# Decoder layer on one core: SyncE gets a list of its own, five x buffers in place of three, and new orders for the first stage

## The reference

```
x1  = layernorm(x  + attention(x))       # linear attention with a memory M, z; 128-wide head; causal sums
x2  = layernorm(x1 + convolution(ctx, x1))
out = layernorm(x2 + ffn(x2))            # y / rms(y) inside
```

```
kv = einsum('bhil,bhjl->bijhl', k_, v_)            # heads of 8, 32 heads
y  = irfft(rfft(kv) * rfft(ssm_kernel))[..., :L]   # causal convolution over L
out = einsum('bijhl,bhil->bjhl', y + kv * D, q_)
```

## Time and profile before

| | |
|---|---|
| median of 3 timed runs | 579.14 us (578.35 to 579.87) |
| the profiled execution | 574.02 us |
| its span, first to last instruction | 572.3 us |
| PE busy | 526.1 us, 92% of the span |
| ACT, POOL, DVE busy | 414.4 us (72%), 388.8 us (68%), 383.4 us (67%) |
| mean granted TensorE clock | 0.984 of full speed |

### The profile page before, as it was taken

How to read it: one execution, slowest core, us unless ns; L and a number is a source line. 1 busy time by engine, 2 the same in 40 slices (tenths; PEclk the granted TensorE clock), 3 DMA queues, 4 the chain that set the end, 5 groups by cost and what they waited for, 6 DMA issues and landing times.

```text
span 572.3 us, 11933 instructions
## 1 busy us (share of the span) xinstructions
PE 526.1 (92%) x3798; PEld 396.7 (69%) x3798; DVE 383.4 (67%) x1153; ACT 414.4 (72%) x978; POOL 388.8 (68%) x449
## 2 busy tenths in 40 slices
PE   5897997996999799999999999999999999998992
PEld 4686785875777467767876777687678767765660
DVE  3984665877776457787777768767877777763223
ACT  3474672535789568878897898788778968887980
POOL 2896762596287538976996798499769967972231
PEclk9998998999999899999999999999999999999997
DMA  9214233403022513012210311040121102001001
GB/s 234 74 52 140 74 115 107 129 1 92 2 75 88 133 50 98 3 57 77 89 47 11 110 55 55 20 145 0 55 81 65 37 0 75 2 1 37 2 19 37
DMA packets 26594, 36.44 MB, mean 64 GB/s; under 512 B 4474, under 2 KB 13818, under 8 KB 26554
## 3 DMA queue, kind: packets, MB, share of 16 engines
q1 hardware_dynamic: 26554, 35.94, 20.8%
HBM read 27.46 MB, written 8.47 MB: 63 GB/s over the span
## 4 chain that ended last, share of the span: by engine, by line
PE 78%; ACT 6%; DVE 6%; DMA 4%; issue 4%; SPq 1%; POOL 1%; POOLq 0%; DVEq 0%; ACTq 0%
PE p_cv L141 7%; PE p_cv L143 7%; PE p_cv L142 7%; PE p_n L1277 6%; PE p_n L1279 6%; PE p_n L1278 6%; PE p_qk L1264 5%; PE p_qk L1266 5%; PE p_x L1264 5%; PE p_ct L99 4%; PE p_x L1266 4%; PE p_s L1266 3%; PE p_s L1264 3%; PE p_qk L890 3%; DMA x_rows<-ring 2%
## 5 line engine op out<-in xcount | busy, mean ns | idle before, releaser
L1122 ACT ACTIVATE p_qk<-p_qk,rescale 128x256 f32<-128x256 f32 x192 | 78.7, 454 | 27.5 <-PE p_qk L1266 27.2
L141 PE MATMUL p_cv<-kv_hi,toe 128*128 128x288 f16 x320 | 92.0, 287 | 6.5 <-issue 6.5
L143 PE MATMUL p_cv<-kv_hi,toe 128*128 128x288 f16 x320 | 92.1, 288 | 0.0
L142 PE MATMUL p_cv<-kv_lo,toe 128*128 128x288 f16 x320 | 92.0, 287 | 0.0
L1090 POOL TENSOR_TENSOR h_lo<-w,h_hi 128x256 f16<-128x256 f32 x88 | 59.4, 682 | 45.2 <-ACT h_hi L1139 44.6
L300 POOL TENSOR_TENSOR shared<-shared 128x1024 f32<-128x1024 f32 x32 | 75.5, 2360 | 16.7 <-DVE shared L260 16.6
L1122 ACT ACTIVATE p_x<-p_x,rescale 128x256 f32<-128x256 f32 x192 | 79.0, 458 | 6.2 <-PE p_x L1266 5.5
L1264 PE MATMUL p_qk<-x_hi,wg_hi 128*128 128x256 f16 x256 | 63.0, 273 | 6.3 <-ACT p_qk L1122 3.3
L226 DVE TENSOR_TENSOR kv_lo<-kv,kv_hi 128x1152 f16<-128x1152 f32 x32 | 60.5, 1889 | 11.6 <-ACT kv_hi L190 10.8
L1277 PE MATMUL p_n<-wd_hi,h_hi 128*128 128x512 f16 x176 | 67.0, 381 | 0.5 <-POOL h_lo L1090 0.5
L1278 PE MATMUL p_n<-wd_lo,h_hi 128*128 128x512 f16 x176 | 67.0, 380 | 0.0
(11 more groups left out here) (162 smaller groups left out, 1300.0 us busy)
## 6 DMA issues: line engine op xcount, KB each, us to landing
toe<-toeplitz_rows SPq DMA_DIRECT2D x16, 512.0 KB, 3.7
ring<-in_x SPq DMA_DIRECT2D x8, 512.0 KB, 3.8
cnat<-in_ctx SPq DMA_DIRECT2D x16, 256.0 KB
x_rows<-ring SPq DMA_DIRECT2D x8, 512.0 KB, 2.8
xq<-x_rows SPq DMA_DIRECT2D x16, 256.0 KB
xr<-x_rows SPq DMA_DIRECT2D x16, 256.0 KB
out_x<-fin SPq DMA_DIRECT2D x16, 256.0 KB
shared<-in_L_ffn_gate_up_packed SPq DMA_DIRECT2D x1, 704.0 KB, 6.9
```

The lines of the kernel that those rows point to most:

```text
L141: nc.tensor.matmul(dst, hi, kh, start=(mb == 0), stop=False)
L142: nc.tensor.matmul(dst, hi, kl, start=False, stop=False)
L143: done = nc.tensor.matmul(dst, lo, kh, start=False, stop=(mb == lb))
L1122: done = nc.scalar.activation(sums, sums, ACT.Copy, scale=rescale[:, p - 1, part * GI + i:part * GI + i + 1])
```

## The change

Three things. First, the ring of x buffers has five instead of three: buffers 3 and 4 are `z3` and `fin`, which the feed-forward first writes at the end of period 1. Its first `add_residual` now also waits for store-3, its first `finish` for store-4. Second, SyncE gets a list START_SYNC, with steps x (load of x), st (store), tw (store of the Toeplitz table), cx (ctx), toe, xq and xr; in each the number is 2 x group + half, except in x and st, where it is the slot. It holds also what `body(1, late=False)` did. Every step waits for what it needs itself. Third, the four other START lists have a new order. The lists of periods 2 to 8 are as before.

```diff
-    ring = [sb(f"ring{k}", [P, 2, D], F32) for k in range(3)]
+    ring = [sb(f"ring{k}", [P, 2, D], F32) for k in range(3)] + [keep["z3"], keep["fin"]]
...
         def load_x(i):
-            wait(sp, x1_stored[i % 3], 16 * (i // 3))
-            sp.dma_start(ring[i % 3][:], tokens(x, i)).then_inc(in_x[i % 3], 16)
+            wait(sp, x1_stored[i % RING], 16 * (i // RING))
+            sp.dma_start(ring[i % RING][:], tokens(x, i)).then_inc(in_x[i % RING], 16)
...
-        for i in range(SLOTS):
-            store_x1(i)
-            if i + 3 < SLOTS:
-                load_x(i + 3)
...
+        def step(s):
+            name, i = named(s)
+            g, p = i // 2, i % 2
+            if name == "x":
+                load_x(i)
+            elif name == "st":
+                store_x1(i)
...
+            elif name == "cx":
+                sp.wait_ge(cv.ctx_reversed, i - 1)
+                load_ctx(g, p)
+            elif name == "toe":
+                if g == 0:
+                    sp.wait_ge(rows_stored, 16)
+                    sp.wait_ge(wts_flipped, 4)
+                else:
+                    sp.wait_ge(cv.convolved, 8 * (i - 1))
+                load_toe(g, p)
...
+        for s in order:
+            step(s)
+        for i in range(4, SLOTS):
+            sp.wait_ge(x1_stored[i % RING], 16 * (i // RING + 1))
...
-        body(1, late=False)
+        store(0, 0)
...
+            if isinstance(f, int) and f == 0:
+                dve.wait_ge(*free[4])
...
+            if isinstance(f, int) and f == 0:
+                dve.wait_ge(*free[5])
...
+    START_SYNC = ("cx2 x3 x4 st0 x5 cx3 tw0 toe1 st1 toe0 x6 st2 st3 xq0 xq1 xr1 x7 xr0 xq3 toe2 cx4 xq2 xq5 st4 xr3 "
+                  "cx5 xr2 toe3 xq4 toe4 st5 cx6 st6 toe5 st7 cx7").split()
...
-                "c10 Xa7 T5 c11 Oa5 Ob5 c12 S6 c13 q2 V6 c14 rt0 c15 Xb7 M6 N6 Q7 q3 rt1 T6 Oa6 +c0 S7 xt0 Ob6 +c1 "
+                "c9 T5 c10 c11 Oa5 rt0 c12 Ob5 c13 c14 V6 c15 S6 q2 M6 Xb7 N6 q3 Q7 rt1 T6 +c0 +c1 Oa6 xt0 Ob6 S7 xt1 "
```

More of the change, by code:

```diff
@@ L35 @@
 HEADS = [groups[0] for groups in PHASES]
+RING = 5
 LATE = ("y1", "n1", "a1", "b1", "e1")
@@ L371, in first_stage @@
     in_sc, in_pg, in_pd, in_k = sem("in_sc"), sem("in_pg"), sem("in_pd"), sem("in_k")
-    in_x = [sem(f"in_x{k}") for k in range(3)]
-    x1_stored = [sem(f"x1_stored{k}") for k in range(3)]
+    in_x = [sem(f"in_x{k}") for k in range(RING)]
+    x1_stored = [sem(f"x1_stored{k}") for k in range(RING)]
     ident_made, masks_made, ones_made, consts = sem("ident_made"), sem("masks_made"), sem("ones_made"), sem("consts")
@@ L400, in tile, with on_sync @@
         return ("g", n) if n < OG else ("d", n - OG)
-    def on_sync(sp):
+    def on_sync(sp, order):
         rows = bass.AP(toeplitz_rows.tensor, 0, [[4 * 640, 16], [1, P], [640, 4], [1, D]])
         def load_x(i):
-            wait(sp, x1_stored[i % 3], 16 * (i // 3))
-            sp.dma_start(ring[i % 3][:], tokens(x, i)).then_inc(in_x[i % 3], 16)
+            wait(sp, x1_stored[i % RING], 16 * (i // RING))
+            sp.dma_start(ring[i % RING][:], tokens(x, i)).then_inc(in_x[i % RING], 16)
         def store_x1(i):
             sp.wait_ge(x1_made, 2 * i + 2)
-            sp.dma_start(tokens(x1_rows, i), ring[i % 3][:]).then_inc(x1_stored[i % 3], 16)
+            sp.dma_start(tokens(x1_rows, i), ring[i % RING][:]).then_inc(x1_stored[i % RING], 16)
         def load_ctx(g, p):
@@ L479, in on_sync @@
-        for k in range(3):
-            sp.wait_ge(x1_stored[k], 16 * ((SLOTS - 1 - k) // 3 + 1))
+        def step(s):
[5 more added lines that the diff above has]
+                store_x1(i)
+            elif name == "tw":
+                sp.wait_ge(kernel_split, 4)
+                sp.dma_start(toeplitz_rows, kpad[:]).then_inc(rows_stored, 16)
+            elif name == "cx":
[8 more added lines that the diff above has]
+                load_toe(g, p)
+            else:
+                for k in range(4):
+                    sp.wait_ge(x1_stored[k], 16)
+                if name == "xq":
+                    if g > 0:
+                        sp.wait_ge(cv.q_flipped, i - 1)
+                    load_rows(cv.xq, cv.in_xq, g, p)
+                else:
+                    if g > 0:
+                        sp.wait_ge(cv.x2_summed, i - 1)
+                    load_rows(cv.xr, cv.in_xr, g, p)
@@ L606, in normalize @@
             for e in range(2):
-                r = ring[i % 3][:, e, :]
+                r = ring[i % RING][:, e, :]
                 nc.scalar.activation(r, r, ACT.Identity, scale=rs[:, i, e:e + 1],
@@ L782, in statistics @@
                 dve.wait_ge(z_made, 2 * i + e + 1)
-                nc.vector.bn_stats(st[:, i, e, :], ring[i % 3][:, e, :]).then_inc(stats, 1)
+                nc.vector.bn_stats(st[:, i, e, :], ring[i % RING][:, e, :]).then_inc(stats, 1)
             for e in range(2):
@@ L879, in flip_x @@
                     done = flip(p_x[:, (k * 2 + e) * P:(k * 2 + e + 1) * P],
-                                ring[i % 3][:, e, (2 * half + k) * P:(2 * half + k + 1) * P])
+                                ring[i % RING][:, e, (2 * half + k) * P:(2 * half + k + 1) * P])
             done.then_inc(x_flipped, 1)
@@ L998, in on_tensor @@
         return step
-    free = [(sq_made, SLOTS), (xT_kept, 2 * SLOTS), (oT_kept, SLOTS), (z_made, 2 * SLOTS)]
+    free = [(sq_made, SLOTS), (xT_kept, 2 * SLOTS), (oT_kept, SLOTS), (z_made, 2 * SLOTS), (x1_stored[3], 16),
+            (x1_stored[4], 16)]
     return (on_sync, on_tensor, on_vector, on_scalar, on_pool), free
@@ new lines, in decoder_layer @@
+    START_PE = ("iw0 Xa0 iw1 Xb0 iw2 iw3 iz0 Q0 V0 S0 M0 Xa1 N0 Xb1 f0 w0 w1 w2 Q1 Xa2 T0 w3 f1 Oa0 w4 Ob0 w5 w6 V1 "
[8 rows of a table added]
+                "+g8_3 +g10_2 +g9_3 +y0_6 +qt1 +g10_3 +d1 +y0_7 +xt0 +y0_8 +y0_9 +y0_10 +xt1").split()
+    START_DVE = ("is0 fs0 sg0 u0 mk0 ig0 dn0 u1 o0 u2 ra0 rb0 sg1 bn0 mk1 dn1 o1 u3 ra1 rb1 sg2 bn1 mk2 nb0 dn2 o2 u4 "
[5 rows of a table added]
+                 "+gu8 +nm0 +gu9 nb5 +gu10 nb6 +nm1 +xt0 bn7 +a0 nb7 +b0 +xt1 +e0").split()
+    START_ACT = ("kw0 xa0 kw1 xb0 ks0 kw2 kw3 re0 vk0 ge0 xa1 rv0 xb1 wh0 lc0 wh1 rv1 kt0 re1 ok0 wh2 wh3 wh4 wh5 wh6 "
[8 rows of a table added]
+                 "+n0 nm6 +xt1 nm7").split()
@@ L1420, in _ @@
             def _(sp):
-                first[0](sp)
+                first[0](sp, START_SYNC)
                 rest[0](sp)
```

51 lines of the change are left out of this document (8 added, 43 removed), and 40 rows, old and new, of tables (START_ACT, START_DVE, START_PE).

## The result

| | before | after |
|---|---|---|
| median of the timed executions | 578.75 us (577.38 to 579.87) | 551.03 us (550.28 to 551.09) |
| profiled execution, its span | 574.02, 572.3 us | 551.09, 549.4 us |
| granted clock of the profiled span | 0.984 | 0.990 |

The ratio is 0.9519, 95% interval 0.9496 to 0.9542. The change makes the kernel 27.7 us faster; I had forecast 15.4, and 551.0 lies under the whole range. The terms of the waits for loads were mostly fair; what failed is the account of what else could be gained.

A forecast was written before the change was run, and what follows sets the result against it. PE was taken as the bound, interrupted by few, large waits. The terms 12.34 + 5.04 + 1.5 - 0.5 - 1.5 - 1.5 = 15.4 us, off 579.14, gave 563.7 us; the range was 557.5 to 572.

The forecast's parts named there:

- SyncE's waits: First stage and period 1: five PE waits on DMA loads, 12.34 us, and half clock behind three, 5.04 us, go.
- query rows' wait: PE ahead of q0: 2.47 us wait and 1.70 of clock go, less 0.5 for a wait that may be left.
- x-3 alone: PE's wait for the x-3 load, issued behind store-0: 3.33 us and 1.64 of clock go, 4.97 us.
- rival E: "Issue" waits might not be Toeplitz loads, x rows held by something else: about 572 us, or 579; chance 0.04.
- x-5 behind store-0: Load x-5 now waits for store-0; slot 5 begins about two slots later, so its cost was counted at nothing.
- In small pieces, 10.24 us: PE's idle time in first stage and period 1 besides the start and named waits; no gain counted in the forecast.
- rt1: End of group 0 on PE: rt1's 1.48 us wait for a copy of q3 goes, counted as 1.5.
- rival C: First stage and period 1: some 6 us of PE's small idle pieces go too, about 557.5 us; chance 0.12.
- The end of period 1: Slot 7's statistics and root ahead of `ms` add 1.5 us on PE, bounds 0 to 3.8; wait 1.21 to about 2.7.
- Rival B: Start of period 2: ctx load behind a store holds ACT's first rescale, PE stands, plus 4.3 us, 568; chance 0.10.
- cover lost: Other engines' work done during PE's three long gaps must fit beside PE's work: 1.5 us of new waits, bounds 0 to 8.
- rivals A and D: A, chance 0.18: gain partly given back as new engine waits, 571 us; D, 0.06: convolution steps wait for DVE, 583 us.

The follow-up runs named there:

- SyncE's part alone: Kernel before with the change's SyncE list and five x buffers, the other four engines' orders as before: 562.4 us, repeated at 561.4 us.
- The buffers' edit: Kernel before with five x buffers, x loads 3 and 4 first in SyncE's list, Toeplitz loads and other engines' orders unchanged: 568.1 us, ratio 0.984.
- The Toeplitz edit: Kernel before with three x buffers and all its orders, only Toeplitz loads 2, 3, 4 moved ahead of stores 5, 6, 7: 567.1 us, ratio 0.983.
- four buffers: Changed kernel with four x buffers instead of five, x loads 4, 5, 6 behind stores 0, 1, 2: 557.4 us, ratio 0.965.

## Why the prediction was wrong

**SyncE's waits: right in the sum.** Their terms were 12.34 + 5.04 = 17.4 us; SyncE's part alone measured 13.9 and 16.4, with half of the query rows' wait left and new half-clock stretches in other places. The buffers' edit gave 8.3 where x-3 alone had 4.97: in its profile half of the query rows' wait went too, and the clock price behind the last wait did not come. The Toeplitz edit gave 9.2, forecast 8.24. "Issue" was indeed the Toeplitz loads (rival E is out). That x-5 behind store-0 costs nothing was right: it was issued at 55.91, and TensorE first reads it at 70.23. With four buffers x-4 has that place, and TensorE asks for it at 58.6, some 12 us sooner.

**The failed step: what else could go.** "In small pieces, 10.24 us" was treated as fixed, and with it the rest of TensorE's busy time. The 10.24 us hold the last wait of 1.21; without it they are 9.0, and the same count in the kernel after is 5.9. So 3.1 us of small waits went. The busy time without the clock losses fell by 3.6 us, from 177.8 - 5.1 = 172.7 to 169.1, with equal instructions. These two are 6.7 of the 7.5 us by which the gain between the profiles (22.9) is over the forecast. The orders were worth 10.4 us by themselves, 6.2 ahead of the first convolution, where I had counted 1.5 for rt1 and part of the 4.17 for the query rows. It was rival C, to which I gave 0.12 and 6 us.

The busy part stood in no row of idle time. The groups of lines seem to show where, SyncE's part alone first, then the kernel after (busy, mean ns | idle before), each from 16 us to period 2:

```profile
L947 PE MATMUL p_n<-woT,oT 128*128 128x512 f32 x32 | 17.3, 642 | 0.5 <-ACT oT L594 0.5
```

```profile
L947 PE MATMUL p_n<-woT,oT 128*128 128x512 f32 x32 | 15.8, 596 | 0.1
```

But the 46 ns each, 1.5 us in all, are mostly half clock. Two pairs of these matmuls in SyncE's part alone, both behind its wait of 1.93 us:

```profile
32.09 1.91 PE L947 MATMUL p_n<-woT,oT 128*128 128x512 f32 x2
...
34.65 1.27 PE L947 MATMUL p_n<-woT,oT 128*128 128x512 f32 x2
```

The trace has single matmuls of 1061, 1061 and 837 ns there and mostly of 592 elsewhere: 1.2 of the 1.5 us. What is left is that the first matmul of a group takes 697 ns four times in the old order and once in the new. Such short pauses, which count as busy, are found all over. By an estimate from the start times of single matmuls at full rate, what lies between two starts beyond the fastest fifth of that shape adds up to 8.9 us in the profile before, 6.9 and 7.2 in the two of SyncE's part alone, and 4.5 in the kernel after. The largest share is that of the weight tiles' transposes, 2.1 us before and 1.0 after. Which moved step took which pause no run shows. The slow start is not in the difference of 3.6 us, since the first Q projection took 3.72 us in both profiles; against SyncE's part alone it is 0.9 and 1.5 us.

**The second failed step: the scale.** I carried the 5.1 us between the profiled and the timed executions over unchanged. By the granted clocks above, most of that is clock lost, a price that each execution draws anew and that comes behind short waits; the change takes most of these waits away, and its executions lie within 1 us of each other. This is 4.8 of the 12.3 us that I missed (22.9 of gain between the profiles, 27.7 between the medians). Some of it is luck of the draw: the first median of the kernel before rests on four executions. In the set with eleven beside the changed kernel the gain was 577.15 - 550.97 = 26.2 us.

**The end of period 1: right in size, and incomplete.** The wait at period 2's first matmul grew from 1.21 to 2.09, where I had said 2.7. I left out the clock behind it (1.7), and ScalarE's reversal was released by a DMA, which I had said would prove me wrong. Store-5 was issued at 177.35 and the ctx half right behind it; its data came 5.2 us later. The Trainium skill ("DMA: Bandwidth & Descriptors", section "Queues, rings and completion order") has each DMA engine take descriptors in ring order. The trace fits that, but how long the same load takes with nothing ahead of it no run shows. Rival B had place and cause right, and its price was nothing alone, since the low half was as late.

**New waits: wrong.** The 1.5 us for cover lost, and the 0.5 left on the query rows, did not come; nor did rivals A and D. The other engines' lists were rearranged with TensorE's, and the busiest of them up to period 2, VectorE, works 141.6 of 182.3 us in the stretch shown; that this room is why the cover was not missed is my reading, and untested.

## What to carry to other kernels

When an order is replaced everywhere, count as gainable all idle time of the engine that bounds, small waits, pauses inside its busy time and the half clock behind them included; here the list of named waits was nearer the floor of the gain than its middle. Spread between executions of one kernel is a term of its own: set span beside granted clock, and ask whether the change takes away the waits behind it. Two waits that end at nearly the same place can hide each other's price (here 0 and 1.6 us alone, 2.6 together): try them together before either is called free. And before a longer mean is put down to an order, look whether some of its instructions ran at half clock.

## What the runs showed of the hardware

- The half-clock stretch (1.2 of 2.4 GHz, 1.7 us lost each time) follows waits shorter than those ahead of the stretches in the earlier trace rows: it came behind the wait of 1.93 us near 30 us in four of five profiles, behind what was left of the query rows' wait in two of three (1.37 and 1.53 us; not behind 1.23), and behind 1.48 us, with short waits around it, in one of seven. It is not certain either: behind the wait of 2.1 us at period 2's start it came in two profiles of the changed kernel and in none of three others that have that wait, and behind 2.52 us (four buffers) and once behind 3.21 (buffers alone) it stayed away.
- TensorE's start varies by itself. With the start order of before, the first Q projection of 16 matmuls took 3.72 us in two profiles, where it began by 10.8, and 4.00 to 5.19 in five, where it began at 11.6 to 11.9, though the page grants 1.00 there. With the new order it began at 10.3 to 11.1 and took 3.72 to 3.83 in all seven. The matmuls before it show when the engine came to full rate: four transposes took 1.06 us still at 10.75 in SyncE's part alone, and 0.60 from 9.48 on with the buffers alone. This line is of the buffers alone, beside those of 11.89 and 11.77 above:

```profile
10.75 3.72 PE L891 MATMUL p_qk<-xT,wT 128*128 128x256 f32 x16 [0.24 <-ACT xT L566]
```
